# One 1024-element scan per slot for four states, a softplus in two batches and a new order on TensorE, in a fused scan and FFN kernel

## What is computed

```python
xb    = silu(conv(x_br));  Bm = xb @ W_b;  Cm = xb @ W_c
delta = softplus(xb @ W_delta + b_delta)
A_bar = exp(delta[..., None] * A)
Bx    = delta[..., None] * Bm[:, :, None, :] * xb[..., None]
h     = a_t * h + bx_t            # over time, for each channel and state
y_t   = sum(h * c_t[:, None, :], axis=-1)
out   = ((y + xb * Dp) * silu(z)) @ W_out + residual
```

## Time and profile before

| | us |
|---|---|
| median of 3 runs | 2953.82 (2953.04 to 2955.74) |
| profiled execution, device time | 2949.14 |
| its span, first to last instruction | 2947.1 |
| of it, until the first scan | 116.7 |
| 16 steps with a scan | 2310 |
| one such step, from one scan0 to the next | 143.96 |
| FFN phase | the last 500 |

### The profile page before, as it was taken

The page is one execution under the profiler, slowest core; times in us unless marked ns, Lnnn a source line. Parts: engine busy times, 40 slices in busy tenths (PEclk is TensorE's granted clock), DMA queues, the critical chain, the costliest instruction groups (busy, mean ns, idle before and its releaser), DMA issues. The chain is left out here.

```text
span 2947.1 us, 38192 instructions
## 1 busy us (share of the span) xinstructions
PE 2391.9 (81%) x11488; PEld 1667.0 (57%) x11520; DVE 2534.0 (86%) x3859; ACT 1802.6 (61%) x3377; POOL 1561.7 (53%) x1321
## 2 busy tenths in 40 slices
PE   7777878788888887878787878787878685899997
PEld 5565656565656565657565656565656331444443
DVE  2499999999999999999999989898999683588887
ACT  2657576666667666757575757575857344456554
POOL 0266666666666565656565656565656460222221
PEclk8888989898989899999898989898998896999999
DMA  4101020102020101010110101010102441211110
GB/s 168 65 1 68 5 68 5 69 5 68 5 69 12 65 14 60 16 58 35 39 44 29 56 18 57 16 59 15 58 8 87 183 153 47 68 63 64 64 54 26
DMA packets 44521, 152.07 MB, mean 52 GB/s; under 512 B 5141, under 2 KB 6037, under 8 KB 41246
## 3 DMA queue, kind: packets, MB, share of 16 engines
q1 hardware_dynamic: 44318, 149.63, 14.3%
HBM read 132.24 MB, written 17.37 MB: 51 GB/s over the span
## 5 line engine op out<-in xcount | busy, mean ns | idle before, releaser
L759 DVE TENSOR_TENSOR_SCAN ring<-a_ps,carry,ring 128x256 f32<-128x256 f32 x2048 | 1363.4, 729 | 44.0 <-ACT a_ps L588 44.0
L391 POOL TENSOR_TENSOR ring<-ring,Cbc 128x1024 f32<-128x1024 f32 x512 | 1208.4, 2360 | 44.2
L588 ACT ACTIVATE a_ps<-delta,nA 128x256 f32<-128x256 f32 x2048 | 853.4, 464 | 458.5 <-DVE ring L759 457.3
L953 PE MATMUL yT_ps<-ident,ring 128*128 128x128 f32 x4096 | 596.1, 296 | 219.3 <-POOL ring L391 203.8
L953 PEld LDWEIGHTS yT_ps<-ident,ring 128*128 128x128 f32 x4096 | 514.7, 153 | 316.0 <-POOL ring L391 239.7
L749 DVE TENSOR_TENSOR ring<-u_ps,Bbc 128x1024 f32<-128x1024 f32 x512 | 619.4, 1212 | 82.7 <-PE yT_ps L953 75.6
L386 POOL TENSOR_TENSOR carry<-ring,half 128x4 f32<-128x4 f32 x512 | 149.6, 292 | 846.8 <-DVE ring L759 846.8
L920 PE MATMUL work<-xb,big 128*128 128x256 f32 x2048 | 491.0, 394 | 63.5 <-ACT zs L470 63.5
L920 PEld LDWEIGHTS work<-xb,big 128*128 128x128 f32 x2048 | 393.3, 198 | 119.6 <-ACT zs L470 67.9
L893 PE MATMUL work<-y0s,big 128*128 128x256 f32 x1024 | 242.9, 395 | 0.7 <-issue 0.7
L936 PE MATMUL work<-Wout,xb 128*128 128x512 f32 x512 | 239.2, 606 | 0.0
(11 more groups left out here) (183 smaller groups left out, 2661.7 us busy)
## 6 DMA issues: line engine op xcount, KB each, us to landing
Bbc<-bc_rows SPq DMA_DIRECT2D x64, 512.0 KB, 4.5
Cbc<-bc_rows SPq DMA_DIRECT2D x64, 512.0 KB, 3.7
xT<-in_xT SPq DMA_DIRECT2D x16, 514.0 KB, 3.3
x_rows<-x2row SPq DMA_DIRECT2D x32, 256.0 KB, 2.0
big<-in_f_w SPq DMA_DIRECT2D x2, 4096.0 KB, 17.5
xp<-x_rows SPq DMA_DIRECT2D x32, 256.0 KB, 2.7
xx<-in_x SPq DMA_DIRECT2D x32, 256.0 KB, 3.0
out_rows<-orow SPq DMA_DIRECT2D x32, 256.0 KB, 2.0
```

The costliest lines, as they stand in the source:

```text
L391: nc.gpsimd.tensor_tensor(h, h, Cbc[:, G * g:G * g + G, :], ALU.mult).then_inc(s_hc, 1)
L588: r = nc.scalar.activation(a_ps[q % 2][:, i, :], delta[:, par, dt, :], ACT.Exp, scale=nA[:, dt, s:s + 1])
L759: r = dve.tensor_tensor_scan(ring[:, q % RING, i, :], a_ps[q % 2][:, i, :], ring[:, q % RING, i, :], carry[:, par, dt, s:s + 1], ALU.mult, ...
L953: r = pe.matmul(yT_ps[:, tt, :], ring[:, q % RING, i, P * tt:P * tt + P], ident[:, :], is_transpose=True, start=False, stop=(g == NG - 1 a ...
```

## The change

One scan of 1024 elements now runs through the four states of a slot. That the states do not run into each other is arranged by data: the first column of a is set to zero once (ACT writes only columns 1 to 255 from then on), and the first column of B*u is the whole first state. For this u has a one in its first column, and the first column of the broadcast B is overwritten for each channel tile with first = exp(delta0*A)*carry + delta0*xb0*B0, by one-element sums on DVE (`tensor_reduce` from `first`): four per step for tile 0, one for each other tile, 11 in all. GpSimd prepares `first` in two halves (`first_col`, `first_sum`, slots 28 and 30 for the next step's tiles 0 to 3, 9 and 11 for tiles 4 to 7), with one Exp on ACT (`first_exp`), and SP writes and reads back 16 numbers B0 per step.

The softplus runs over four tiles at a time (two batches in place of four), its second batch in slots 3 to 6 of the next step. scan0 reads its second input from PSUM in place of SBUF. On PE, turn(q-1) stands first in every slot; wo(1) moves from slot 6 to slot 8, z(3) from 24 to 17, and dl(0) and dl(1) fill slots 20 to 23. On DVE, stats(0) is in slot 7 and stats(1) in slot 8 (both were in slot 8). On ACT, silu moves from slot 19 to 17 and zsilu from 30 to 21. The last eighth of one FFN weight is loaded after the last one-element sum, since `first` lies in its place.

```diff
+NCOL = NG + ND - 1
+FIRST = (28, 9)
...
+        spare = big[0][:, 7 * DI:8 * DI]
+        B0 = spare[:, 0:2 * NS].rearrange("p (b s) -> p b s", b=2)
+        a0 = spare[:, 64:64 + ND // 2 * NS].rearrange("p (d s) -> p d s", s=NS)
+        u0 = spare[:, 128:128 + ND // 2]
+        first = spare[:, 256:256 + ND * NS].rearrange("p (d s) -> p d s", s=NS)
...
-            eng.wait_ge(s_delta, 4 * k + dt // 2 + 1)
+            eng.wait_ge(s_delta, 2 * k + dt // (ND // 2) + 1)
...
+                    sp.dma_start(b0_dram[bpar].rearrange("(n o) -> n o", o=1), bcs[0:NS, 0:1]).then_inc(s_bcw, 16)
                     sp.dma_start(bc_dram[bpar], bcs[:, :]).then_inc(s_bcw, 16)
-                    sp.wait_ge(s_bcw, 16 * n + 16)
+                    sp.wait_ge(s_bcw, 32 * n + 32)
+                    wait(sp, s_first, 2 * n - 2)
+                    sp.dma_start(B0[:, bpar, :], b0_dram[bpar:bpar + 1, :].to_broadcast([P, NS])).then_inc(s_b0l, 16)
...
+            def first_col(half, n, bp):
+
+                if half == 0:
+                    pool.wait_ge(s_b0l, 16 * n + 16)
+                pool.wait_ge(s_delta, 2 * n + half + 1)
+                pool.wait_ge(s_xb, 2 * n + half + 1)
+                wait(pool, s_first, 2 * n + half)
+                lo, hi = ND // 2 * half, ND // 2 * half + ND // 2
+                d0 = delta[:, bp, lo:hi, 0:1]
+                nc.gpsimd.tensor_tensor(a0[:, :, :], d0.to_broadcast([P, ND // 2, NS]), nA[:, lo:hi, :], ALU.mult)\
+                    .then_inc(s_a0, 1)
+                nc.gpsimd.tensor_tensor(u0[:, :].rearrange("p (d o) -> p d o", o=1), d0, xb[:, bp, lo:hi, 0:1], ALU.mult)\
+                    .then_inc(s_a0, 1)
+                wait(pool, s_col0, NCOL * (n - 1) + (NG + ND // 2 - 1 if half == 0 else NCOL))
+                pool.wait_ge(s_a0, 4 * (2 * n + half) + 2)
+                nc.gpsimd.tensor_tensor(first[:, lo:hi, :], u0[:, :].rearrange("p (d o) -> p d o", o=1)
+                                        .to_broadcast([P, ND // 2, NS]),
+                                        B0[:, bp, :].rearrange("p (d s) -> p d s", d=1).to_broadcast([P, ND // 2, NS]),
+                                        ALU.mult).then_inc(s_a0, 1)
+
+            def first_sum(half, n, bp):
+
+                lo, hi = ND // 2 * half, ND // 2 * half + ND // 2
+                pool.wait_ge(s_a0e, 2 * n + half + 1)
+                nc.gpsimd.tensor_tensor(a0[:, :, :], a0[:, :, :], carry[:, bp, lo:hi, :], ALU.mult).then_inc(s_a0, 1)
+                pool.wait_ge(s_a0, 4 * (2 * n + half) + 4)
+                nc.gpsimd.tensor_tensor(first[:, lo:hi, :], first[:, lo:hi, :], a0[:, :, :], ALU.add)\
+                    .then_inc(s_first, 1)
+
             def step(k, par, front, back, scan):
                 for q in range(NQ):
                     dt, g = q // NG, q % NG
                     if front and q == 8:
                         rstd(k + 1)
+                    if scan and q == FIRST[1]:
+                        first_col(1, k, par)
+                    if scan and q == FIRST[1] + 2:
+                        first_sum(1, k, par)
+                    if front and q == FIRST[0]:
+                        first_col(0, k + 1, 1 - par)
+                    if front and q == FIRST[0] + 2:
+                        first_sum(0, k + 1, 1 - par)
...
-                    for j in range(NT * DI // 512):
+                    for j in (2, 3):
...
-                             15: [lambda: xcopy(1)], 16: [lambda: xcopy(2)], 17: [lambda: xcopy(3)],
-                             18: [lambda: zcopy(0)], 19: [lambda: zcopy(1), silu], 21: [lambda: zcopy(2)],
-                             22: [bc], 25: [lambda: dexp(0, False)], 26: [lambda: dln(0, False)],
-                             27: [lambda: dexp(1, False)], 28: [lambda: dln(1, False), lambda: zcopy(3)],
-                             30: [zsilu], 32: [lambda: dexp(2, False)]}
-                scan_plan = {2: [lambda: dln(2, True)], 3: [lambda: dexp(3, True)], 4: [lambda: dln(3, True)]}
+                             15: [lambda: xcopy(1)], 16: [lambda: xcopy(2)], 17: [lambda: xcopy(3), silu],
+                             18: [lambda: zcopy(0), lambda: zcopy(1)], 19: [lambda: zcopy(2), lambda: zcopy(3)],
+                             21: [zsilu], 22: [bc], 24: [lambda: dexp(0, False)], 25: [lambda: dexp(1, False)],
+                             26: [lambda: dln(0, False)], 32: [lambda: dexp(2, False)]}
+                scan_plan = {3: [lambda: dexp(3, True)], 6: [lambda: dln(1, True)]}
                 back_plan = {6: [lambda: gT(ND // 2 - 1, fp)], 9: [lambda: wout(0)], 11: [lambda: wout(1)]}
                 for q in range(NQ + 1):
                     dt, g = q // NG, q % NG
+                    if scan and q == FIRST[1] + 2:
+                        first_exp(1, k)
+                    if front and q == FIRST[0] + 2:
+                        first_exp(0, k + 1)
...
-                        r = nc.scalar.activation(a_ps[q % 2][:, i, :], delta[:, par, dt, :], ACT.Exp,
+                        r = nc.scalar.activation(a_ps[q % 2][:, i, 1:T], delta[:, par, dt, 1:T], ACT.Exp,
...
+                    dve.wait_ge(s_tanh, n + 1)
+                    dve.scalar_tensor_tensor(ps[0:N0, T:2 * T], ps[0:N0, T:2 * T], V[0:N0, V_BS:V_BS + 1], e0[:, :],
+                                             ALU.add, ALU.mult).then_inc(s_c0, 1)
+                    dve.wait_ge(s_c0, base + 3)
+                    dve.tensor_tensor_scan(st0[:, :], sc0[0:N0, 3:4].to_broadcast([N0, T]), ps[0:N0, T:2 * T],
+                                           carry0[:, fp:fp + 1], ALU.mult, ALU.add).then_inc(free[BANK["PRJ"]], 1)
...
+                    if g == 0 and dt in (0, ND // 2):
+                        dve.wait_ge(s_first, 2 * k + (2 if dt else 1))
+                    if dt == 0:
+                        dve.tensor_reduce(Bbc[:, G * g:G * g + G, 0], first[:, 0, G * g:G * g + G]
+                                          .rearrange("p (s o) -> p s o", o=1), AX.X, ALU.add).then_inc(s_col0, 1)
+                        dve.wait_ge(s_col0, NCOL * k + g + 1)
+                    elif g == 0:
+                        dve.tensor_reduce(Bbc[:, :, 0], first[:, dt, :].rearrange("p (s o) -> p s o", o=1), AX.X, ALU.add)\
+                            .then_inc(s_col0, 1)
+                        dve.wait_ge(s_col0, NCOL * k + NG + dt)
                     dve.tensor_tensor(ring[:, q % RING, :, :],
                                       u_ps.rearrange("p (a t) -> p a t", a=1).to_broadcast([P, G, T]),
                                       Bbc[:, G * g:G * g + G, :], ALU.mult).then_inc(s_bx, 1)
...
                     dt, g = q // NG, q % NG
                     dve.wait_ge(s_a, NQ * k + q + 1)
                     dve.wait_ge(s_bx, NQ * k + q + 1)
-                    for i in range(G):
-                        s = G * g + i
-                        r = dve.tensor_tensor_scan(ring[:, q % RING, i, :], a_ps[q % 2][:, i, :],
-                                                   ring[:, q % RING, i, :], carry[:, par, dt, s:s + 1],
-                                                   ALU.mult, ALU.add)
-                    r.then_inc(s_scan, 1)
-
-                next_plan = {4: [gates0], 5: [scan0], 8: [stats], 13: [keep_y0],
-                             24: [lambda: dmin(0, False)], 25: [lambda: dmax(0, False)],
-                             26: [lambda: dmin(1, False)], 27: [lambda: dmax(1, False)]}
-                scan_plan = {0: [lambda: dmin(2, True)], 2: [lambda: dmax(2, True), lambda: dmin(3, True)],
-                             4: [lambda: dmax(3, True)]}
+                    dve.tensor_tensor_scan(ring[:, q % RING, :, :].rearrange("p g t -> p (g t)"),
+                                           a_ps[q % 2][:, :, :].rearrange("p g t -> p (g t)"),
+                                           ring[:, q % RING, :, :].rearrange("p g t -> p (g t)"), 0.0,
+                                           ALU.mult, ALU.add).then_inc(s_scan, 1)
+
+                next_plan = {4: [gates0], 5: [scan0], 7: [lambda: stats(0)], 8: [lambda: stats(1), stats_end],
+                             13: [keep_y0], 25: [lambda: dmin(0, False)], 27: [lambda: dmax(0, False)]}
...
+                        dve.memset(u_ps[:, 0:1], 1.0).then_inc(s_aclr, 1)
+                        dve.wait_ge(s_mxc, ND)
+                        for i in range(2):
+                            dve.memset(a_ps[i][:, :, 0:1], 0.0).then_inc(s_aclr, 1)
...
-                        5: [("n", wo, 0), ("b", wout, 0, 1)], 6: [("b", wout, 0, 2), ("n", wo, 1)],
-                        7: [("b", wout, 1, 0)], 8: [("b", wout, 1, 1)], 9: [("b", wout, 1, 2), ("n", turn_y0)],
-                        10: [("n", turn_back)],
+                        5: [("n", wo, 0), ("b", wout, 0, 1)], 6: [("b", wout, 0, 2)],
+                        7: [("b", wout, 1, 0)], 8: [("n", wo, 1), ("b", wout, 1, 1)],
```

(14 more changed lines are left out.)

78 lines of the change are left out of this document (45 added, 33 removed).

## The result

The changed kernel takes **3053.64 us** (median of 5 runs, 3037.89 to 3058.31), the kernel before 2953.04 beside it (5 runs): ratio 1.0338, 95% interval 1.0308 to 1.0367, so 3.4% slower. The forecast was 3009 in a range of 2920 to 3070. The profiled run of the changed kernel took 3037.89 us (span 3035.8, mean granted clock 0.903 as before); it is the lowest of the five, 16 us under their median. In the experiments, one run of silu19 (3568.61 us, granted clock 0.66) and one of the kernel before beside it (3284.37 us, 0.73) fell in a slow state, and without them the two medians are 2997.02 in place of 2998.12 and 2952.91 in place of 2953.17.

The account below looks back on a forecast made before the run. VectorE was taken as the bound, TensorE second. From 2949.1 us, 15 steps at +4.8, -9 for the last step and -8 before the first scan gave 3004, or 3009 as a median; range 2920 to 3070.

Parts of the forecast that it names:

- rivals on the scan: DVE's long scan no cheaper (2.58 us; about 3100 us, chance 0.10) or far cheaper (1.47; about 2820, chance 0.06).
- third bound: DVE's long scan: with the product's 0.13 us as fixed part it would take 2.4 us, saving 6 per step.
- -10.8 us of own work: DVE's work per step: long scan -11.0, scan0 -1.6, one-element sums +2.1, softplus -0.3 us.
- A: Slot 8: DVE waits 4.8 us before stats(1), for wo(1) behind turn(7) and POOL's product of slot 7.
- B: Slot 10: DVE waits 5.5 us for exponentials behind y0scale, turn_y0, wout and turn(8); 4.3 at full clock.
- C: Slot 13: DVE's gate needs turn(11), behind PE's x(0); a wait of 2.0 us.
- D: Slot 17: DVE waits 4.9 us for PE's x jobs, then ACT's xcopy(3), silu, two table loads and exponentials.
- E: Slot 21: zsilu with two table loads on ACT, between two slots' exponentials; DVE waits 1.5 us.
- F: Slots 20 to 23: PE's dl jobs and turns outlast DVE's slots, dmin(0) in slot 25 needs them; 3 us.
- G: Slot 26: ACT's load, Ln, load and exponentials behind a late dmin; DVE waits 1.7 us.
- +4.8 us per step: Whole step: waits rise by 15.6 us, DVE's own work falls by 10.8, so the step gets 4.8 us longer.
- jobs come in time: Rival: slot 13 and later waits stay at today's 3.4 us, a step saves 7.1, kernel 2831 us; chance 0.14.

Follow-up runs that it names:

- silu19: The changed kernel with silu on ScalarE back in slot 19 in place of slot 17: 2998.12 us, ratio 1.0146.
- stats6: The changed kernel with stats(0) on VectorE in slot 6 in place of slot 7: 3030.14 us, ratio 1.0266.
- wo7: The changed kernel with wo(1) on TensorE in slot 7 in place of slot 8: 2977.56 us, ratio 1.0081.
- turns_last: The changed kernel with TensorE's turns behind each slot's jobs again, except in slots divisible by 4: 2940.49 us, ratio 0.9962.
- mended: The changed kernel with wo(1) in TensorE's slot 7, silu in ScalarE's slot 19, stats(0) in VectorE's slot 6: 2898.19 us, ratio 0.9819.
- replaced: The changed kernel, turns still first, with nearly every job of the front given a new slot: 2757.71 us, ratio 0.9337.

## Why the prediction was right, and by how much it was off

The sign, the mechanism and all seven places were as forecast; the median came out 45 us above it, inside the range. Of these, 11 us are the runs' own: the profiled run lies 16 under its median, before 5. By the prediction's own steps:

**A long scan at 2.24 us to the next start**: 2.20. That 2.1 ns are a column holds: (2.28 - 0.667) / 768 = 2.10. The fixed part was given as 0.19; with a start value in SBUF it is that (2.339 for 1024, 0.727 for 256), with a constant it is 0.13. The sum was right to 1.3 us per step, for a reason partly missed: the saving was put down to the merging alone, and the runs show most of it in the start value. The rivals on the scan (2.58, 1.47) are excluded. The third bound, the product's 0.13 as the fixed part, was added up wrongly: it gives 2.44 and 4.5 us saved, not 2.4 and 6.

**scan0 at 0.74**: 739 ns. **The one-element sums at 0.2 each**: 0.20 and 0.22 to the next start.

**-10.8 us of own work**: -8.9. This is the step that failed. scan0's wait for GpSimd was booked as a gain and closed; it went in part to y0's instruction (+0.67), and stats(0) in slot 7 made a new one at u (+2.07). stats6 shows the second, in which DVE works 1.8 less. The prediction had no term for either. The softplus saved 0.7 where 0.3 was forecast (minima and maxima together 4.4 us per step before, 3.75 now).

**Waits of 24.4**: the brackets add up to 23.1, with two small ones to 23.9, and each lies near its price, in the step shown and in the mean:

| | forecast | step shown | mean of 14 | shown by |
|---|---|---|---|---|
| A | 4.8 | 4.74 | 5.01 | wo7: gone |
| B | 5.5 | 5.32 | 5.03 | turns_last: gone |
| C | 2.0 | 2.11 | 2.33 | turns_last: gone |
| D | 4.9 | 1.36 + 3.33 | 1.36 + 3.33 | silu19: the 3.33 goes |
| E | 1.5 | 1.12 | 1.17 | turns_last: gone |
| F | 3 | 3.35 | 3.31 | turns_last: 1.27 |
| G | 1.7 | 1.79 | 1.79 | turns_last: 0.49 |

D was written as one chain from x to silu. It is two waits: the gate's turn behind x (1.36, in all of wo7, silu19 and mended) and silu with its loads. Their sum was right. For B the low clock was taken to follow from A's idle stretch. In the step shown it came later: TensorE idles 3.55 and 0.75 us before turn(8), whose eight transposes then take 1.97 where they took 1.09 above, and six wout records 3.22 where six took 2.74 at 1060.26. The granted clock is 1.00 from 1058 to 1063, 0.76 from 1066 to 1068 and 0.50 in the 2 us after.

```profile
1066.55 0.43 PE L1027 MATMUL yT_ps<-ident,xdp 128*128 128x128 f32 x2 [3.55 <-DVE gbuf L774]
1067.73 1.97 PE L1032 MATMUL yT_ps<-ident,ring 128*128 128x128 f32 x8 [0.75 <-POOL ring L447]
1069.49 3.22 PE L1015 MATMUL work<-Wout,xb 128*128 128x512 f32 x6
```

That is 1.4 us more in B's chain, and the sum at full clock was 4.3. In the next step the low clock comes earlier, 0.73 and 0.70 from 1209 to 1215, and then it is A that is long (wo takes 1.48 where it took 1.02, A 5.20) while B is 4.01. wo7, with 1.00 from 1166 to 1186, has B at 4.02. So B at full clock is 4.0, and what the low clock adds falls now on A and now on B; the prediction gave it to B and called A the same "whatever the rest does". C, E, F and G were not taken apart by a run of their own; turns_last moves them all at once.

**+4.8 us per step**: 7.1 from scan0 to scan0 (14 steps in the trace). 1.9 of the difference is the work above.

**-9 for the last step, -8 before the first scan**: -15.2 and -3.9. The last step, from its first scan to its last, takes 143.8 us where it took 159.1: 12.6 less work of DVE, where 11 was put in, and 2.6 less waiting, where a wait or two more was put in. The first scan starts at 112.8 where it started at 116.7, half of what was taken. Between these two lie the 15 steps with a front, 150.6 us each where they took 143.4: 107.5 us in all, against 15 x 4.8 = 72. With 0.3 behind the last scan this makes the +89 of the profiled run, where +55 was forecast. So the steps were 35 too cheap and the two ends together 2 too dear.

**The range**, 2920 to 3070, does not follow from its terms. B at 4.3, C at 0.5 and F and G at half take 5.05 us off a step, which gives 2933; the scan at 2.4 adds 5.1, which alone gives 3086. The measured 3054 lies inside either way.

**The rival "jobs come in time"**, 2831 us, did not happen here; mended, three jobs moved by a slot or two, comes to 2898, 67 us short of it, and replaced (2758) that the same instructions can do better than that rival. For this the table of slots mattered more than the scan: from the changed kernel to replaced 296 us, while the scan in replaced is worth 129.5.

**Not settled**: why the changed kernel's profiled run lies 16 us under its median, so that the medians of it and of stats6 are 23 us apart and their profiled runs 10; and how much of replaced comes from TensorE's clock (0.95 against 0.90 over 14 steps), since no run moved the clock alone. No run undid the softplus in two batches, the first columns or scan0's input in PSUM by itself; that scan0 is short because of this input rests on its rows before and after.

## What to carry to other kernels

When an engine gets shorter work, ask of every job that another engine does for it in a fixed slot whether its distance still suffices: here 8.9 us per step were saved and 15.4 lost, in waits whose length could be summed from rows. An order (turn first or last) has no worth of its own: the same edit gave -23, +113 and -115 us with three placements of the jobs. When an instruction stops waiting for a shared resource, look which instruction is the next to ask for it.

## What the runs showed of the hardware

- A VectorE scan costs 60 ns more when its start value is read from SBUF instead of given as a constant: 727 against 667 ns at 256 columns, 2339 against 2280 at 1024. A column costs 2.10 ns in either form.
- VectorE instructions with two SBUF inputs that met a product on GpSimd lasted until it was over: scan0 0.74 to 2.33, u 0.41 to 2.48, y0's 0.47 to 1.13. Ones with a single SBUF input did so too: nrm (128x2) took 0.17 us in the changed kernel and 1.81 in wo7, and dmin, a minimum with a constant, took 0.69 us in the changed kernel and 2.00 in the row shown of turns_last, where it ended 0.56 behind a product of GpSimd (1226.16 to 1228.52). The Trainium skill (SBUF — State Buffer, section Who interferes with whom) names this form as well, tensor_scalar in a mode with two ports, an exception that the prediction's sentence on this page left out. No row here states an instruction's mode. The long scan, with one input in PSUM, never shows it: 2280 ns in the mean of 512, 2292 at most.
- TensorE's granted clock was 0.90 over 14 steps with 25 us of DVE waits each and 0.95 over 14 with 6, and the same matmuls then took 116.7 and 111.0 us per step. DVE's waits alone do not set it: the kernel before had 9 us of them and 0.90 as well.
